# Mixing matrices made on VectorE, and their transfers on GpSimd's queue, from sample 4 on

## The reference

```
x = x + conv(x, weight, 4 groups) + (cond @ c_weight.T)[:, :, None] + bias
att = softmax(mlp(cond))                       # 64 x 8
agg_w = einsum('bk,koi->boi', att, weight8)    # one 128x128 matrix per sample
x = x + einsum('boi,bih->boh', agg_w, x) + (att @ bias_k)[:, :, None]
```

## Time and profile before

| | |
|---|---|
| median of 3 runs | 724.07 us (723.28 to 730.01) |
| profiled execution | 725.75 us, span 723.6 us |
| PE busy | 713.3 us, 99% |
| ACT busy | 598.6 us, 83% |
| POOL busy | 546.6 us, 76% |
| DVE busy | 465.5 us, 64% |
| granted clock of TensorE | 0.999 of full |
| moved | 177.56 MB, 245 GB/s over the span |

### The profile page before, as it was taken

The page is one execution under the profiler, slowest core; times in us unless marked ns, Lnnn a source line. Parts: engine busy times, 40 slices in busy tenths (PEclk is TensorE's granted clock), DMA queues, the critical chain, the costliest instruction groups (busy, mean ns, idle before and its releaser), DMA issues.

```text
span 723.6 us, 29229 instructions
## 1 busy us (share of the span) xinstructions
PE 713.3 (99%) x12419; PEld 622.5 (86%) x12419; DVE 465.5 (64%) x413; ACT 598.6 (83%) x456; POOL 546.6 (76%) x592
## 2 busy tenths in 40 slices
PE   8999999999999999999999999999999999999996
PEld 6899998998888888888888888888888888888885
DVE  6987667577777666566566566566566566576543
ACT  5988887888888888888888888888888888888843
POOL 2899999999999999866766766766766766767740
PEclk9999999999999999999999999999999999999999
DMA  6445867867876867887787778678768777777546
GB/s 225 158 151 183 285 229 241 286 201 268 283 248 230 293 237 254 281 271 255 249 291 258 241 262 287 225 250 275 268 225 294 245 249 269 243 249 270 191 156 239
DMA packets 66551, 177.56 MB, mean 245 GB/s; under 512 B 7437, under 2 KB 50008, under 8 KB 50264
## 3 DMA queue, kind: packets, MB, share of 16 engines
q1 hardware_dynamic: 66002, 176.93, 71.4%
q10 hardware_dynamic: 518, 0.17, 0.1%
HBM read 101.57 MB, written 75.50 MB: 245 GB/s over the span
## 4 chain that ended last, share of the span: by engine, by line
PE 82%; POOL 11%; DMA 4%; issue 1%; SPq 1%; DVE 0%; ACT 0%; DVEq 0%; POOLq 0%; ACTq 0%
PE ps L432 61%; PE ps L463 21%; POOL mix_prod L755 4%; POOL mix_prod L750 4%; DMA mix_dram<-mix_parts 2%; POOL mix_sum_f L758 2%; DMA mix_rep<-mix_dram 1%; DMA x_in<-in_x_dram 1%; POOL mix_f L762 1%; SPq L291 1%; POOL mix_parts L768 1%; POOL mix_parts L765 0%; ACT x_hi L515 0%; POOL par L745 0%; POOL par L774 0%
## 5 line engine op out<-in xcount | busy, mean ns | idle before, releaser
L432 PE MATMUL ps<-x_hi,cw_hi 32*128 32x512 f32 x3072 | 384.8, 385 | 0.9 <-ACT x_hi L515 0.6
L432 PE MATMUL ps<-x_hi,cw_lo 32*128 32x512 f32 x3072 | 384.1, 384 | 0.0
L511 ACT ACTIVATE x_ph<-x_in 128x2560 f32<-128x2560 f32 x63 | 318.6, 5058 | 2.7 <-DMA x_in<-in_x_dram 2.1
L613 DVE TENSOR_TENSOR y_lo<-ps,y_hi 128x512 fp32r<-128x512 f32 x256 | 159.2, 684 | 239.1 <-ACT y_hi L524 239.1
L432 PE MATMUL ps<-x_lo,cw_hi 32*128 32x512 f32 x3072 | 274.7, 385 | 0.0
L432 PEld LDWEIGHTS ps<-x_lo,cw_hi 32*128 32x128 f32 x3072 | 222.1, 183 | 21.1 <-issue 0.8
L463 PE MATMUL ps<-y_hi,mix_rep 32*128 32x512 f32 x2048 | 214.4, 385 | 1.6 <-DMA mix_rep<-mix_dram 1.6
L432 PEld LDWEIGHTS ps<-x_hi,cw_hi 32*128 32x128 f32 x3072 | 195.3, 183 | 22.6 <-issue 1.7
L432 PEld LDWEIGHTS ps<-x_hi,cw_lo 32*128 32x128 f32 x3072 | 194.8, 183 | 20.3 <-issue 0.2
L537 ACT ACTIVATE z_out<-ps,par 128x1024 f32<-128x1024 f32 x124 | 146.1, 1236 | 75.3 <-PE ps L463 75.3
L602 DVE TENSOR_TENSOR x_lo<-x_ph,x_hi 128x2560 fp32r<-128x2560 f32 x63 | 189.4, 3007 | 2.2
(11 more groups left out here) (80 smaller groups left out, 92.7 us busy)
## 6 DMA issues: line engine op xcount, KB each, us to landing
x_in<-in_x_dram SPq DMA_DIRECT2D x64, 1024.0 KB, 7.3
out_dram<-z_out SPq DMA_DIRECT2D x63, 1024.0 KB, 5.0
mix_rep<-mix_dram SPq DMA_DIRECT2D x256, 128.0 KB, 2.6
mix_dram<-mix_parts SPq DMA_DIRECT2D x64, 128.0 KB, 7.0
out_dram<-x_in SPq DMA_DIRECT2D x2, 512.0 KB, 3.5
z_out<-in_L_cond_weight_dram SPq DMA_DIRECT2D x1, 512.0 KB, 3.9
cw_nat<-in_L_cond_weight_dram SPq DMA_DIRECT2D x1, 144.0 KB, 2.2
w_sb<-in_L_cond_W_dram ACTq DMA_DIRECT2D x2, 64.0 KB, 5.1
```

What stands on the lines that cost most here:

```text
L432: mm = pe.matmul(y_at(s)[:, g, :], w[rows, m, :], x_at(xx[buf(s)], rows, m), start=i == 0, stop=i == CONV - 1)
L511: nc.scalar.activation(x_ph[buf(s)][:, :, :, :], by_lane(x_in[buf(s)]), ACT.Copy).then_inc(x_split_ph, 1)
L613: nc.vector.tensor_tensor(y_lo[s[1]][:, g, :], y_at(s)[:, g, :], y_hi[s[1]][:, g, :].bitcast(F32), ALU.subtract).then_inc(y_lo_made, 1)
```

## The change

Up to sample 3 nothing moves: GpSimd makes the matrices, SP stores and loads them. From sample 4 on (`FIRST`) VectorE makes the matrix, in slot s behind the rests of y, with another order of operations: two running sums, over the even and the odd terms, the identity in the odd one; their sum twice (once in fp32, once rounded to the high part), and the rest. The matrix of sample 63 is made in the slot of sample 62, behind that of 62. GpSimd's slot s then holds the store of the matrix of s and, when it has landed, its four loads, on GpSimd's own queue, each group behind a one-element addition (`gate`) that carries order. SP keeps x and z.

```
+FIRST = 4
 # SP: store_mix, load_mix return at once unless number(s) < FIRST
 # PE: first mix step waits for mix_loaded_soft instead of mix_loaded from sample 4 on
 # DVE
+            def mix_matrix(s):
+                if not exists(s) or by_pool(s):
+                    return
+                at_least(dve, z_read, done(s, 2, lag=-U))
+                if is_sample(s, FIRST):
+                    dve.wait_ge(par_made, FIRST)
+                a = par[s[1]]
+                nc.vector.tensor_copy(a[:, :], table[:, number(s), :]).then_inc(par_made, 1)
+                dve.wait_ge(par_made, done(s))
+                for k in range(NK):
+                    part = (mix_even, mix_odd)[k % 2]
+                    if k == 0:
+                        nc.vector.tensor_scalar(part[:, :], mixw_t[:, k, :], a[:, k:k + 1], None,
+                                                ALU.mult).then_inc(mix_term, 1)
+                        continue
+                    if k >= 2:
+                        dve.wait_ge(mix_term, done(s, NK, lag=-FIRST - 1) + k - 1)
+                    nc.vector.scalar_tensor_tensor(part[:, :], mixw_t[:, k, :], a[:, k:k + 1],
+                                                   ident[:, :] if k == 1 else part[:, :],
+                                                   ALU.mult, ALU.add).then_inc(mix_term, 1)
+                dve.wait_ge(mix_term, done(s, NK, lag=-FIRST))
+                nc.vector.tensor_tensor(mix_f[:, :], mix_even[:, :], mix_odd[:, :], ALU.add).then_inc(mix_sum, 1)
+                if is_sample(s, FIRST) or is_sample(s, FIRST + 1):
+                    dve.wait_ge(mix_stored[buf(s)], DMA * uses(s))
+                else:
+                    dve.wait_ge(mix_stored_soft[buf(s)], DMA * uses_soft(s))
+                nc.vector.tensor_tensor(mix_parts[buf(s)][:, 0, :], mix_even[:, :], mix_odd[:, :],
+                                        ALU.add).then_inc(mix_sum, 1)
+                dve.wait_ge(mix_sum, done(s, 2, lag=-FIRST))
+                nc.vector.tensor_tensor(mix_parts[buf(s)][:, 1, :], mix_f[:, :],
+                                        mix_parts[buf(s)][:, 0, :].bitcast(F32),
+                                        ALU.subtract).then_inc(mix_made, 1)
+                dve.wait_ge(mix_made, done(s, lag=-FIRST))
             def slot(s):
                 ...
                 for g in range(G):
                     rest_y(s, g)
+                if not is_sample(s, NS - 1):
+                    mix_matrix(s)
+                if is_sample(s, NS - 2):
+                    mix_matrix(after(s, 1))
 # POOL
+            def store_mix(s):
+                if not exists(s) or by_pool(s):
+                    return
+                b = buf(s)
+                pool.wait_ge(mix_made, done(s, lag=-FIRST))
+                ...
+                    pool.wait_ge(mix_loaded_soft[b], DMA * G * uses_soft(s))
+                at_least(pool, passed, done(s, 2, lag=-FIRST - 1))
+                nc.gpsimd.tensor_tensor(gate[:, 0:1], ident[0:1, 0:1], ident[0:1, 0:1], ALU.add).then_inc(passed, 1)
+                pool.dma_start(mix_dram[b][:, :, :], mix_parts[b][:, :, :].bitcast(F32)).then_inc(mix_stored_soft[b], DMA)
+            def load_mix(s):
+                if not exists(s) or by_pool(s):
+                    return
+                b = buf(s)
+                pool.wait_ge(mix_stored_soft[b], DMA * (uses_soft(s) + 1))
+                if not is_sample(s, NS - 1):
+                    pool.wait_ge(z_ready, done(s, PH, lag=-2))
+                pool.wait_ge(passed, done(s, 2, lag=-FIRST - 1) + 1)
+                nc.gpsimd.tensor_tensor(gate[:, 1:2], ident[0:1, 0:1], ident[0:1, 0:1], ALU.add).then_inc(passed, 1)
+                for r in range(PH):
+                    pool.dma_start(rep_at(s)[Q * r:Q * r + Q, :, :, :].bitcast(F32).rearrange("c g h o -> c g (h o)"),
+                                 mix_dram[b].rearrange("(g c) h o -> c g (h o)", g=G)).then_inc(mix_loaded_soft[b], DMA)
+            def slot(s):
+                if by_pool(s):
+                    mix_matrix(s)
+                store_mix(s)
+                load_mix(s)
```

More of the change, by code:

```diff
@@ L116, in cond_resid_kernel @@
         mix_sum_f = sb("mix_sum_f", [P, P])
+        mix_f_first = sb("mix_f_first", [P, P])
+        gate = sb("gate", [1, 2])
+        mix_even = sb("mix_even", [P, P])
+        mix_odd = sb("mix_odd", [P, P])
         mix_f = sb("mix_f", [P, P])
@@ L205, in cond_resid_kernel @@
         prod_made = sem("prod_made")
+        tree_sum = sem("tree_sum")
+        mix_hi_made = sem("mix_hi_made")
+        mix_first_made = sem("mix_first_made")
+        mix_term = sem("mix_term")
+        passed = sem("passed")
         mix_sum = sem("mix_sum")
-        mix_hi_made = sem("mix_hi_made")
         mix_made = sem("mix_made")
@@ L210, in cond_resid_kernel @@
         mix_loaded = two(sem, "mix_loaded")
+        mix_stored_soft = two(sem, "mix_stored_soft")
+        mix_loaded_soft = two(sem, "mix_loaded_soft")
         z_ready = sem("z_ready")
@@ L222, in is_sample, with uses_soft, by_pool @@
             return isinstance(s[0], int) and number(s) == b
+        def uses_soft(s):
+            n, k = s
+            return n * (U // 2) + k // 2 - FIRST // 2
+        def by_pool(s):
+            return isinstance(s[0], int) and number(s) < FIRST
         def pipeline(eng, slot):
@@ L269, in store_mix @@
             def store_mix(s):
-                if not exists(s):
+                if not exists(s) or not by_pool(s):
                     return
@@ L274, in store_mix @@
                 made, taken = ahead(done(s), DMA * G * uses(s))
-                sp.wait_ge(mix_made, made)
+                sp.wait_ge(mix_first_made, made)
                 at_least(sp, mix_loaded[b], taken)
@@ L443, in mix_step @@
                     if r == 0:
-                        pe.wait_ge(mix_loaded[buf(s)], DMA * G * (uses(s) + 1))
+                        if by_pool(s):
+                            pe.wait_ge(mix_loaded[buf(s)], DMA * G * (uses(s) + 1))
+                        else:
+                            pe.wait_ge(mix_loaded_soft[buf(s)], DMA * G * (uses_soft(s) + 1))
                     if is_sample(s, 0):
@@ L735, in mix_matrix @@
             def mix_matrix(s):
-                if not exists(s):
-                    return
                 at_least(pool, z_read, done(s, 2, lag=-U))
@@ L755, in mix_matrix @@
                     nc.gpsimd.tensor_tensor(mix_prod[:, 0:half, :], mix_prod[:, 0:half, :],
-                                            mix_prod[:, half:2 * half, :], ALU.add).then_inc(mix_sum, 1)
-                    pool.wait_ge(mix_sum, done(s, 3, lag=-1) + n + 1)
+                                            mix_prod[:, half:2 * half, :], ALU.add).then_inc(tree_sum, 1)
+                    pool.wait_ge(tree_sum, done(s, 3, lag=-1) + n + 1)
                 nc.gpsimd.tensor_tensor(mix_sum_f[:, :], mix_prod[:, 0, :], mix_prod[:, 1, :],
-                                        ALU.add).then_inc(mix_sum, 1)
-                pool.wait_ge(mix_sum, done(s, 3))
-                nc.gpsimd.tensor_tensor(mix_f[:, :], mix_sum_f[:, :], ident[:, :], ALU.add)
+                                        ALU.add).then_inc(tree_sum, 1)
+                pool.wait_ge(tree_sum, done(s, 3))
+                nc.gpsimd.tensor_tensor(mix_f_first[:, :], mix_sum_f[:, :], ident[:, :], ALU.add)
                 at_least(pool, mix_stored[buf(s)], DMA * uses(s))
@@ L767, in mix_matrix @@
                 pool.wait_ge(mix_hi_made, done(s))
-                nc.gpsimd.tensor_tensor(mix_parts[buf(s)][:, 1, :], mix_f[:, :],
+                nc.gpsimd.tensor_tensor(mix_parts[buf(s)][:, 1, :], mix_f_first[:, :],
                                         mix_parts[buf(s)][:, 0, :].bitcast(F32),
-                                        ALU.subtract).then_inc(mix_made, 1)
-                pool.wait_ge(mix_made, done(s))
+                                        ALU.subtract).then_inc(mix_first_made, 1)
+                pool.wait_ge(mix_first_made, done(s))
                 if is_sample(s, 0):
@@ L774, in mix_matrix @@
                     nc.gpsimd.tensor_copy(par[0][:, NK:PC], table[:, 0, NK:PC]).then_inc(par_made, 1)
+            def store_mix(s):
[3 more added lines that the diff above has]
+                pool.wait_ge(mix_made, done(s, lag=-FIRST))
+                if is_sample(s, FIRST) or is_sample(s, FIRST + 1):
+                    pool.wait_ge(mix_loaded[b], DMA * G * uses(s))
+                else:
+                    pool.wait_ge(mix_loaded_soft[b], DMA * G * uses_soft(s))
[14 more added lines that the diff above has]
+                                 mix_dram[b].rearrange("(g c) h o -> c g (h o)", g=G)).then_inc(mix_loaded_soft[b], DMA)
             pool.wait_ge(table_made, 1)
             pool.wait_ge(mixw_copied, 1)
-            pipeline(pool, mix_matrix)
+            def slot(s):
+                if by_pool(s):
+                    mix_matrix(s)
+                store_mix(s)
```

(2 more changed lines are left out.)

## The result

The changed kernel took 754.38 us (median of 6 runs, 752.33 to 757.46) beside 725.12 for the kernel before: ratio 1.0383, interval [1.0352, 1.0413] (the ratios in this text are those on record; the quotient of the two medians is 1.0404). The forecast was 731.3 with a range up to 741. The profiled execution took 757.46 us; its span is 755.4, that of before 723.6, so 31.8 us have to be found.

A forecast was written before the change was run, and what follows sets the result against it. TensorE, busy 713.3 of 723.6 us, was taken to bound the kernel. Early wait gone -1.75, late end +7.3 and lower clock +1.7 make +7.25: 731.3 us against the median of 724.07, range 722 to 741.

The forecast's parts named there:

- Steady slots: Middle of the kernel: matrix needs 12.6 us of a 15.0 lead, GpSimd's round 10.25 against TensorE's 10.88; both hold narrowly.
- +7.25: Whole kernel: sum of -1.75 (early wait gone), +7.3 (late end) and +1.7 (lower clock), in us.
- The stop near sample 4: TensorE's wait for matrix copies at about 120 us, expected to go: -1.75 us.
- one wait: Longest wait of the mix for matrix copies; 1.75 us lost over 55 slots was all assigned to it.
- is worth nothing: SP's x loads and z stores go out earlier, without gain, as TensorE doesn't wait for them.
- c: Time of one transfer issue by GpSimd: taken as 0.9 us, bounded by 0.19 and 1.36.
- the steady way of a matrix: Steady slots: gate 1.8, store 0.9 + 3.5, gate 0.25, four issues 3.8, landing 2.3, together 12.6 us.
- The end: Last two matrices: mix 62 2.8 us late, last mix at 720.85 instead of 713.53, +7.3 us.
- the forecast's own rule: At the end of the kernel, every 0.1 us of c is 1.0 us.
- The clock's +1.7: Last mix starts at 1.2 GHz after TensorE stands for 4.8 us: +1.7 of a possible 4.4 us.
- VectorE's 3.3 us: Twelve instructions a matrix take 3.3 us and fit VectorE's 4.2 free; rival that VectorE bounds: 765 us, chance 0.07.
- GpSimd's round is no bound: Steady slots: GpSimd's round 10.25 us against 10.88; rival that it becomes the bound: about 774 us, chance 0.13.

The follow-up runs named there:

- pad32: The kernel before with one unused 32-byte tensor per partition placed ahead of mix_f, nothing else: 745.07 us, ratio 1.0243.
- end: The changed kernel with its four new tensors allocated behind all others, the work the same: 735.73 us, ratio 1.0095.
- pad64: The kernel before with one unused tensor of 64 bytes ahead of mix_f: 743.63 us, ratio 1.0232.
- dve_sp: The changed kernel with new tensors behind all others and the matrices' store and loads left on SP's queue, GpSimd issuing none: 731.12 us, ratio 1.0061.

## Why the prediction was wrong

- **Steady slots: the step that failed.** The text had "TensorE's slot still 10.88; if it is longer, the idle time before VectorE's y rests (none: VectorE bounds) or before GpSimd's gates (none: its round bounds) says which". It is 11.20, and there is idle time at both places. The forecast took TensorE's own 10.88 as given and gave no reason for it. The added tensors move its weights by 1568 bytes, which is 32 modulo 256: +0.32 us a slot, shown by pad32 (18.6 us by the medians without the change) and end (18.7 less than the changed kernel, with the change). Without this term end is 0.95% of 726.9, 6.9 us, slower (8.8 by the medians), where the forecast had +7.25.
- **That agreement is partly luck.** The stop near sample 4 was to vanish (-1.75). It grew instead: +5.5. The forecast put all of the 1.75 down to one wait, but that wait was 1.1 us (the longest); for the rest TensorE lost time while busy. And it said of SP's x loads and z stores that going out earlier "is worth nothing"; they are what the matrix's transfers then met.
- **GpSimd's issue, c, and the landings were mis-sized**: for c 0.9 was taken, 0.55 to 0.58 is the median (below). The transfers of the changed kernel that GpSimd issued, loads and store, each by its source line (duration min/median/max in ns, first and last start), and behind each its time from issue to landing:

```profile
L865 POOL DMA_DIRECT2D mix_rep<-mix_dram x240: 550/552/1420, 83.1 to 742.0; - x120
...
DMA to landing us min/median/max: 2.6/5.7/8.5
...
L851 POOL DMA_DIRECT2D mix_dram<-mix_parts x60: 576/578/1743, 73.7 to 737.8; - x60
...
DMA to landing us min/median/max: 2.3/2.4/9.2
```

  Counted from the start of its issue the median store lands after 2.4 us, where 0.9 + 3.5 was taken for the steady slots, and the median load after 5.7, where 0.9 + 2.3 was taken. The two errors cancel: the steady way of a matrix, 12.6 in the forecast, is 12.4 for the one ready at 405.19, whose last copy lands at 417.6. So the sum came right, by luck in its parts. In the Trainium skill, "DMA: Bandwidth & Descriptors", Anatomy of one DMA — SWDGE (gpsimd) path, a fixed 2.0 us and 436 GB/s make about 2.3 for these 128 KB by my estimate; the median store agrees, the 9.2 and the loads' 5.7 do not.
- **The end was late in the way forecast, with other sizes.** Mix 62 waited 2.33 us (2.8 forecast). The last mix came 5.1 us late, the slot's 0.2 taken off (7.3 forecast). With c = 0.55 the forecast's own rule, 1.0 us for each 0.1 of c, gives 7.3 - 3.5 = 3.8; the chain was 1.4 longer than that rule makes it (21.1 beside 19.7): the store of matrix 62 took 5.24 us where 0.55 + 2.3 was reckoned, 2.4 more, and the other links were together 1.0 shorter (the store of 63 landed in 2.3). Ahead of the last mix TensorE stood for 0.8 us, not the 4.8 forecast: the two mixes began 5.4 us apart instead of 7.5, and mix 62, mostly at the low level (0.52 granted from 740 to 743), took 4.6 of them instead of 2.7. By the same two points in their chains the last mix is 5.4 late in end and 3.3 in dve_sp: most of it is the late place of the matrices, some 2 us GpSimd's queue. The clock's +1.7 came to 0.1 in the changed kernel (mix 62 had the low level, the last mix 4.49 us), but to 1.5 in end (5.91) and 1.6 in dve_sp (6.02), whose last mix began right behind the stop.
- **Right**: VectorE's 3.3 us (3.2 measured) and that 3.3 fits into its slot; GpSimd's round is no bound. Its gate, 0.18 us alone, has a mean of 1.10 (group L850 above), as VectorE's cast runs beside most of them. In 14 of the 60 samples the gate was through before the cast, and then the issue of the store, which began with the cast or in it, took 1.3 to 1.7 us instead of 0.58 (VectorE and GpSimd, one such place):

```profile
428.04 1.49 DVE L619 CAST x_hi<-x_ph 128x2560 fp32r<-128x2560 f32 x1 [0.61 <-DVE mix_parts L750]
...
427.58 0.19 POOL L850 TENSOR_TENSOR gate<-ident 1x1 f32<-1x1 f32 x1 [4.16 <-DVE mix_parts L750]
428.04 1.61 POOL L851 DMA_DIRECT2D mix_dram<-mix_parts  x1 [0.27 <-issue]
```

  The Trainium skill, "SBUF — State Buffer", SBUF: two separate sides, has GpSimd, and with it the descriptors of its transfers, locked out while VectorE copies or casts in a 2-port mode. The gates and these issues agree, and it cost nothing here. The 1.80 us copy that the forecast held beside this rule is not quite such a case: beside it ran x's rest, a difference of two tensors and not a copy.
- The sum for the 31.8 us, by ScalarE's roundings of y: the first begins 2.0 us later (27.51 beside 25.52); in the other runs it begins anywhere from 24.9 to 28.3, in pad64, which has the long slot, at 24.98, so this is not the slot's. From there to sample 62 it is 24.6 more: 5.5 near sample 4 and 19.1 for the slots, since the first three, 7.3 to 11.6 us long, grew by 0.2 together. The end is 5.25, the last mix 0.1 more, and what follows it 0.15 less.

## What to carry to other kernels

An added tensor is a change to every instruction that reads what lies behind it: put new tensors behind all old ones, and if TensorE's slot changes with unchanged products, test 32 unused bytes first. A queue's order is also a brake: whoever moves a transfer off it must ask what the queue will now send early, and beside what. A late link that is covered by a whole slot in the middle is bare at the end, where no next sample's work covers it.

## What was not expected of the hardware

A step of four TensorE products of 512 columns takes about 7 ns more of its slot (11.20/48 = 233.3 against 10.88/48 = 226.7 ns) when its weights and its moving values start 32 or 64 bytes apart modulo 256, at a granted clock of 1.00, and it does so for either kind of step by itself. The same 128 KB store lands in 2.4 us or in 9 to 10, and in these runs the longest, near sample 4 to 6, are those with a burst of z and x transfers out beside them.
